# Six expert blocks with one shared down product of a weighted slot sum, and four head pieces moved from GpSimd to VectorE

## The chip, the cores and the metric

One core of one Trainium2 chip. The metric is the device time of one execution in microseconds (us), median of the runs given. In each core, TensorE (PE in the profile) does matrix products, VectorE (DVE) and ScalarE (ACT) elementwise work, GpSimd (POOL) slower elementwise work; each engine takes its instructions in the order in which they stand, and they wait for each other by semaphores. Products land in eight PSUM banks of 128 partitions x 512 float32.

## The reference, cut to what matters

A two-layer model on four sequences of 256 tokens by 256 features. Layer 0 has grouped attention (`attn_a`), an expert layer (`ffn`), an attention across the 16 heads of each token (`attn_b`), and the same expert layer again; layer 1 follows with a delta rule, two dense layers and an attention. The change touches the expert layer (called twice per sequence, so eight blocks) and the attention across heads.

```python
# expert layer, 8 experts, 2 of them chosen per token, F = 896, rank 32
rw, sel = top_k(softmax(x @ Wg.T), 2);  rw = rw / rw.sum()
base1 = x @ W1.T;  base3 = x @ W3.T
for k in range(2):
    mask = one_hot(sel[:, k], 8)
    x1 = base1 + lora1(mask);  x3 = base3 + lora3(mask)   # low-rank parts of the chosen expert
    x2 = silu(x1) * x3
    down  = x2 @ W2.T
    lora2 = (mask * (x2 @ A2.T)) @ B2                     # low-rank part of the down product
    out = out + (down + lora2) * rw[:, k]
# attn_b: for each token, softmax over its 16 heads
scores  = einsum('bshd,bstd->bsht', q, k) / sqrt(16)
attn    = einsum('bsht,bstd->bshd', softmax(scores), v)
```

## The kernel before, in words

The four sequences are named a, b, c, d (s = 0 to 3). Activations of a sequence are `X[s]` (2 tiles of 128 tokens x 256) and, transposed and normed, `XnT[s]`. The order of all work stands in one function, `program`: it calls `stage(name, k, s)` once for every step, and each engine runs through the same list and issues only its own part of a step (`table[name]`). So the order of an engine's queue is the order of this list.

**An expert block** (`experts(stage, k, s, beside)`) runs over seven tiles m of 128 of the 896 hidden features. `x_first` m is slot 0: eight products of 256 columns on TensorE, a Silu on ScalarE, a product on VectorE (`product`, result `x2T[s][:, 0, m]`). `x_second` m is slot 1, two steps of m later: four more products onto the same bank (the difference of the low-rank parts), then again Silu and product (`x2T[s][:, 1, m]`). The down products multiply each 128x128 block of `x2T` by 512 columns of `m_down`: 256 are W2, 256 are A2 of all experts. There are 2 slots x 2 token tiles x 7 tiles m = 28 of them. `down` on VectorE adds the W2 half, weighted by `rw`, to `X`, and masks the A2 half by `onehotw` into `am2` / `am2b`, which `lora_t` adds and `lora` multiplies by B2.

**Woven blocks.** In `middle` (once for a and b, once for c and d) two of the blocks run with the attention across heads of the other sequence beside them: block (0, b) with the heads of a, then block (1, a) with the heads of b; likewise (0, d) with c and (1, c) with d. I call the first kind W1 and the second W2; there are two of each. In them slot 0's down products are spread over the loop (`down_sum`), from m = 4 on. `token_heads(s)` says at which step of the block each part of the heads stands: 16 pieces (8 of scores, 8 of mixing, `head_scores` and `head_mix`), each made of a product of 128 x 1024 on GpSimd (`head_prod`) and a sum over 16 on VectorE. GpSimd may be four pieces ahead. The heads' result is transposed and projected on TensorE at the step "down10", behind the first of slot 1's two groups of down products (`head_out_t`, `head_out`).

**The other blocks**: (0, a) stands nearly alone; (0, c) has the first attention of d beside it; (1, b) and (1, d) have the start of the delta rule beside them.

PSUM banks are given out by `Ring`; `lanes` limits which banks a step may take. `claim` waits until the bank's former content is drained. TensorE's clock is granted by the chip; `warm` issues products without use where the engine would otherwise stand idle.

Of the kernel before, what the change touches and what calls it, by code (L numbers as in the profile page):

```python
# [8 lines left out]
ALU = mybir.AluOpType  # L9
# [3 lines left out]
P = 128  # L13
# [10 lines left out]
PIECES = 2 * NT * HP  # L24
NB = 4
# [73 lines left out]
def hybrid_kernel(nc, x_in, masks, packs, where, out):  # L99
    with ExitStack() as ctx:  # L100
# [206 lines left out]
        am_ready = each("am_ready")  # L307
        silu_ready = each("silu_ready")
# [102 lines left out]

        def lanes(name, k, s):
# [6 lines left out]
            if s % 2 == 0:  # L419
                return range(0, 3)  # L420
# [149 lines left out]
        def token_heads(s):  # L570
# [19 lines left out]
        def experts(stage, k, s, beside):  # L590
# [91 lines left out]
        def _(pe):  # L682
# [195 lines left out]

            def x_first(k, sm):
# [29 lines left out]
            def down(k, sia):  # L909
# [6 lines left out]
                for m in range(FT):  # L916
                    if i == 1 and a == 0:
                        wait_drained(pe, ("x", r, m))
                    last = mm(o[:, :], x2T[s][:, i, m, a * P:(a + 1) * P], wd[:, m, :], m == 0, m == FT - 1)
                last.then_inc(full[ring.bank(("down", r, i, a))], 1)  # L920

            def down_sum(k, sm):
# [4 lines left out]
                for a in range(NT):  # L927
                    o = claim(pe, ("down", r, 0, a)) if m == 0 else bank[ring.bank(("down", r, 0, a))]
                    last = mm(o[:, :], x2T[s][:, 0, m, a * P:(a + 1) * P], wd[:, m, :], m == 0, m == FT - 1)
# [296 lines left out]
            table = dict(head_prod=nothing, spread2=nothing, delta_sq=nothing, consts=nothing, top_exp=nothing, ffn_half=ffn_half, delta_expand=nothing, delta_diag=nothing, conv_tap=nothing, gates=nothing, down_sum=down_sum, angles=nothing, norm_x=nothing, norm_t=norm_t, latent=latent, kv=kv, kv_fold=kv_fold,  # L1226
# [19 lines left out]
        def _(act):  # L1246
# [70 lines left out]
            def silu(k, s, i, m):  # L1317
# [11 lines left out]
                act.activation(silu_x[s][:, n % SX, :], psum(key, T), ACT.Silu).then_inc(silu_ready[s], 1)  # L1329

# [163 lines left out]
            table = dict(head_prod=nothing, spread2=nothing, delta_sq=nothing, consts=nothing, top_exp=top_exp_, ffn_half=nothing, delta_expand=nothing, delta_diag=nothing, conv_tap=conv_tap, gates=nothing, down_sum=nothing, angles=angles, norm_x=nothing, norm_t=norm_t, latent=latent, kv=nothing, kv_fold=nothing,  # L1494
# [17 lines left out]
        def _(dve):  # L1512
# [177 lines left out]
            def gates(k, s):  # L1690
# [4 lines left out]
                link(dve.tensor_tensor(rw[s][:, 1, :], rw[s][:, 2, :], rw[s][:, 0, :], ALU.mult))  # L1695
                for a in range(NT):
# [3 lines left out]
                settle()  # L1700

# [32 lines left out]
            def down(k, sia):  # L1734
# [44 lines left out]
            def head_scores(_, sah):  # L1779
# [4 lines left out]
                dve.wait_ge(hprod_ready[s], nth(s, PIECES, p + 1))  # L1784
# [8 lines left out]
            def head_mix(_, sah):  # L1793
# [8 lines left out]
                dve.wait_ge(hprod_ready[s], nth(s, PIECES, p + 1))  # L1802
# [509 lines left out]
```

## Time and profile before

| | us |
|---|---|
| median of 3 runs (lowest, highest) | 1312.7 (1312.7, 1315.37) |
| the profiled execution | 1312.18 |
| its span in the trace | 1310.4 |
| TensorE busy | 1202.5 (92% of the span) |
| VectorE busy | 677.2 (52%) |
| ScalarE busy | 416.9 (32%) |
| GpSimd busy | 229.6 (18%) |

The page gives shares over the whole span; what a change in one stage is worth is read from the stage. The timeline gives every instruction with its start and duration, and in brackets how long its engine had been idle before it and what ended that. A float32 product of 256 or 512 columns shows as two instructions (two matmul records and two weight loads), so "x18" in a row of 128x512 products is nine of them; a transpose shows as one. Durations of single TensorE records overlap, so the price of a product is taken from a long row divided by its count.

### The profile page before, as it was taken

To read this page: it belongs to the slowest core of one execution; us is meant where nothing else is said; L and a number is where in the kernel's file an instruction comes from. 1 tells how busy PE (TensorE), PEld (TensorE's weight loads), DVE (VectorE), ACT (ScalarE), POOL (GpSimd) and SP (SyncE) were. 2 spreads that over 40 slices of the span, in tenths; PEclk is the share of its full clock that TensorE was granted. 3 is DMA by queue.
4 is the path that set the end of the run, shared out by engine and by line. 5 is a ranking of instruction groups with operands and counts; after the bars stand their busy time and mean duration, and the time that the engine had idled before them with its cause. 6 is when DMAs were issued, how large, how long until landed. Compare 5 with 4: busy or idle time off the path is not lost.

```text
span 1310.4 us, 17604 instructions
## 1 busy us (share of the span) xinstructions
PE 1202.5 (92%) x6865; PEld 916.2 (70%) x6865; DVE 677.2 (52%) x1661; ACT 416.9 (32%) x897; POOL 229.6 (18%) x133
## 2 busy tenths in 40 slices
PE   6889999999998989988787999999999989899888
PEld 5677675767866778667565776757678677786666
DVE  5753266664465456334634433666644655663351
ACT  3623021313222342433453431313133223424352
POOL 0000074560110210000000000836501102100000
PEclk9999999999999999989998999999999999998989
DMA  8200000000000000000000000000000000000000
GB/s 350 115 1 1 1 1 1 1 1 1 1 1 2 1 1 1 1 2 9 1 9 1 1 1 1 1 0 1 0 1 1 1 1 1 1 1 2 1 1 17
DMA packets 3570, 17.32 MB, mean 13 GB/s; under 512 B 288, under 2 KB 2464, under 8 KB 2976
## 3 DMA queue, kind: packets, MB, share of 16 engines
q1 hardware_dynamic: 2912, 14.12, 2.7%
q10 hardware_dynamic: 576, 2.08, 0.4%
q8 instruction: 55, 0.90, 0.3%
q14 instruction: 27, 0.22, 0.1%
HBM read 15.15 MB, written 1.05 MB: 12 GB/s over the span
## 4 chain that ended last, share of the span: by engine, by line
PE 70%; DVE 11%; issue 9%; ACT 6%; POOL 2%; DMA 0%; DVEq 0%; POOLq 0%; ACTq 0%
PE bank L684 66%; ACT scr L1278 3%; PE bank L701 2%; DVE XnT L1960 2%; DVE XnT L1962 1%; DVE scr L1552 1%; DVE stat L1544 1%; POOL rstd L2116 1%; DVE negmax L1634 1%; PE bank L802 1%; DVE X L1537 1%; PE bank L1089 1%; ACT scr L1256 1%; POOL fac L2116 1%; ACT XnT L1256 1%
## 5 line engine op out<-in xcount | busy, mean ns | idle before, releaser
L684 PE MATMUL bank<-pack,scr 128*128 128x512 f32 (+2 forms) x944 | 312.1, 483 | 8.5 <-ACT scr L1256 7.5
L684 PE MATMUL bank<-XnT,pack 128*128 128x256 f32 x1024 | 251.3, 385 | 11.9 <-ACT XnT L1256 7.1
L684 PEld LDWEIGHTS bank<-pack,scr 128*128 128x128 f32 x944 | 178.5, 193 | 114.9 <-issue 89.4
L684 PE MATMUL bank<-scr,pack 128*128 128x256 f32 x944 | 227.0, 380 | 1.3 <-DVE scr L1715 1.1
L684 PEld LDWEIGHTS bank<-XnT,pack 128*128 128x128 f32 x1024 | 191.7, 192 | 45.4 <-ACT XnT L1256 9.6
L684 PEld LDWEIGHTS bank<-scr,pack 128*128 128x128 f32 x944 | 178.1, 190 | 30.3 <-issue 4.4
L2138 POOL TENSOR_TENSOR scr<-scr 128x1024 f32<-128x1024 f32 x64 | 149.9, 2379 | 47.3 <-DVEq L1777 46.6
L2116 POOL TENSOR_TENSOR rstd<-veps,half 128x2 f32<-128x2 f32 x32 | 22.3, 698 | 750.2 <-DVE veps L1549 750.2
L1725 DVE TENSOR_TENSOR scr<-bank,scr 128x256 f32<-128x256 f32 x112 | 47.2, 423 | 149.5 <-ACT scr L1329 148.6
L1278 ACT ACTIVATE scr<-bank,negmax 128x256 f32<-128x256 f32 (+1 forms) x256 | 82.9, 445 | 92.5 <-DVE negmax L1634 92.5
L1329 ACT ACTIVATE scr<-bank 128x256 f32<-128x256 f32 x112 | 42.6, 384 | 210.5 <-PE bank L684 210.3
L1256 ACT ACTIVATE scr<-bank 128x512 f32<-128x512 f32 (+7 forms) x112 | 51.0, 474 | 176.8 <-PE bank L701 90.0
L684 PE MATMUL bank<-scr 32*128 32x128 f32 (+4 forms) x944 | 78.8, 322 | 1.3 <-ACT scr L1256 1.3
L684 PEld LDWEIGHTS bank<-scr 32*128 32x128 f32 (+2 forms) x944 | 65.7, 186 | 19.8 <-issue 9.0
L1632 DVE TENSOR_REDUCE negmax<-bank 128x2 f32<-128x512 f32 x64 | 43.8, 684 | 68.0 <-PE bank L684 68.0
L1256 ACT ACTIVATE mats<-bank 128x512 f32<-128x512 f32 (+1 forms) x80 | 42.6, 555 | 106.4 <-PE bank L1089 83.7
L1537 DVE TENSOR_TENSOR X<-bank,X 128x512 f32<-128x512 f32 x31 | 21.4, 691 | 94.2 <-PE bank L684 94.2
L802 PE MATMUL bank<-pack,scr 128*128 128x128 f32 x384 | 55.6, 295 | 8.2 <-ACT scr L1278 7.6
L701 PE MATMUL bank<-pack,scr 128*128 128x128 f32 x232 | 38.0, 292 | 24.5 <-DVE scr L1552 15.6
L684 PE MATMUL bank<-identb 128*128 128x512 bf16 x197 | 55.6, 383 | 5.0 <-DVE scr L1656 3.9
L802 PEld LDWEIGHTS bank<-pack,scr 128*128 128x128 f32 x384 | 46.5, 151 | 14.9 <-ACT scr L1278 11.6
L701 PEld LDWEIGHTS bank<-pack,scr 128*128 128x128 f32 x232 | 28.7, 149 | 39.9 <-issue 20.3
(178 smaller groups left out, 1384.9 us busy)
## 6 DMA issues: line engine op xcount, KB each, us to landing
pack<-pack_dram SPq DMA_DIRECT2D x1, 6152.0 KB, 17.5
pack<-pack_dram SPq DMA_DIRECT2D x1, 2180.0 KB, 29.6
pack<-pack_dram SPq DMA_DIRECT2D x1, 1595.0 KB, 23.5
X<-x SPq DMA_DIRECT2D x4, 256.0 KB, 16.9
pack<-pack_dram SPq DMA_DIRECT2D x1, 1024.0 KB, 20.3
pack<-pack_dram ACTq DMA_DIRECT2D x1, 975.5 KB, 6.3
pack<-pack_dram SPq DMA_DIRECT2D x1, 793.5 KB, 25.0
out_dram<-X SPq DMA_DIRECT2D x3, 256.0 KB, 2.1
```

Source lines behind the costliest of these rows:

```text
L684: return pe.matmul(o, l, r, start=start, stop=stop, skip_group_check=True)
L701: last = pe.transpose(o[:, t * T + a * P:t * T + a * P + P], src(t, a), ident)
L802: last = pe.transpose(o[:, (c - 4 * b) * P:(c - 4 * b + 1) * P], prob[s][:, u % PR, c * P:(c + 1) * P], ident)
L1256: act.activation(dst, src, func, **kw).then_inc(drain_of(key), 1)
L1278: ins = act.activation(prob[s][:, u % PR, j * HW + lo:j * HW + hi], psum(key, BANK)[:, lo:hi], ACT.Exp, bias=negmax[s][:, u % PR, tile, j: ...
L1329: act.activation(silu_x[s][:, n % SX, :], psum(key, T), ACT.Silu).then_inc(silu_ready[s], 1)
L1537: dve.tensor_tensor(xf, psum(key, n), xf, ALU.add).then_inc(drain_of(key), 1)
L1632: dve.tensor_reduce(negmax[s][:, u % PR, 1, 2 * h:2 * h + 2], o[:, :, P:HW], AX.X, ALU.max, negate=True).then_inc(max_ready[s], 1)
L1725: dve.tensor_tensor(x2T[s][:, i, m, :], psum(key, 2, T)[:, 1, :], silu_x[s][:, n % SX, :], ALU.mult)\
L1960: link(dve.tensor_tensor(t, rows16[:, 0:i + 1, :, i].rearrange("p j m -> p m j"), solved(s)[:, :, 0:i + 1], ALU.mult))
L2116: return pool.tensor_tensor(dst, src, half[:, 0:1].broadcast_to(shape) if len(shape) == 2 else half[:, 0:1].unsqueeze(1).broadcast_to(shap ...
L2138: pool.tensor_tensor(prod[s][:, hh], *pairs, ALU.mult).then_inc(hprod_ready[s], 1)
```

## The change

In six of the eight blocks (`joined`: all of k = 0, and (1, a) and (1, c)), the two slots share the W2 half of the down product. With rw0 and rw1 the weights and r = rw1 / rw0, the sum x2(0) + r x2(1) is formed in place of x2(1) and slot 1's down products take it; their result is weighted by rw0. Slot 0's 14 down products keep only the A2 half (256 columns instead of 512), and the mask of slot 0 becomes (onehot0 - onehot1) rw0, that of slot 1 onehot1 rw0, so that the A2 parts come out the same.

For this, `ratio_rows` copies r along 256 columns on VectorE at m = 0, TensorE turns it into rows with two products of 128 columns (`ratio`, behind `x_first` 1), ScalarE copies them to `ratio_t`, and GpSimd multiplies x2(1) by it and adds x2(0), two instructions of 128x256 for each m (`x_second` on GpSimd). The down products of slot 1 wait for `sum_ready`. VectorE no longer adds slot 0's part to `X` (two instructions fewer per block), and `gates` has one instruction more.

In the heads, the last four of the sixteen pieces (`AHEAD = 12`) get their product on VectorE right before its sum; GpSimd makes the first twelve. Two of the steps at which pieces stand are moved by one.

```diff
 PIECES = 2 * NT * HP
+AHEAD = PIECES - HP
...
+        def joined(k, s):
+            return k == 0 or s % 2 == 0
...
-                slots = ["f3", 3, "f4", 4, 4, "f5", 5, 5, "f6", 6, 6, "f7", 7, 7, 8, 8]
+                slots = ["f3", 3, "f4", 4, 4, "f5", 5, 5, "f6", 6, 6, "f7", 7, "f8", 8, 8]
...
-                slots = [1, "f2", 2, "f3", 3, 3, "f4", 4, "f5", 5, 5, "f6", 6, 6, "f7", 7]
+                slots = [1, "f2", 2, "f3", 3, 3, "f4", 4, "f5", 5, 5, "f6", 6, "f7", 7, "f8"]
...
-                if p + HP < len(pieces):
+                if p + HP < AHEAD:
                     beside[slot].append(("head_prod", 0, (s, p + HP)))
...
             for m in range(FT + 2):
+                if m == 0 and joined(k, s):
+                    stage("ratio_rows", k, s)
                 if m < FT and (m or (k == 0 and s % 2 == 0)):
                     stage("x_first", k, (s, m))
+                if m == 1 and joined(k, s):
+                    stage("ratio", k, s)
...
+            def ratio(k, s):
+                pe.wait_ge(ratio_ready[s], nth_sum(k, s, 1, 1))
+                o = claim(pe, ("ratio", (k, s)))
+                for a in range(NT):
+                    last = mm(o[:, a * P:(a + 1) * P], ratio_w[s][:, a, :], ident, True)
...
-                    last = mm(o[:, :], x2T[s][:, i, m, a * P:(a + 1) * P], wd[:, m, :], m == 0, m == FT - 1)
+                    if i == 1 and a == 0 and joined(k, s):
+                        pe.wait_ge(sum_ready[s], nth_sum(k, s, FT, m + 1))
+                    c0 = D if i == 0 and joined(k, s) else 0
+                    last = mm(o[:, c0:2 * D], x2T[s][:, i, m, a * P:(a + 1) * P], wd[:, m, c0:2 * D],
+                              m == 0, m == FT - 1)
...
+                if p < AHEAD:
+                    dve.wait_ge(hprod_ready[s], nth(s, AHEAD, p + 1))
+                else:
+                    wait_drained(dve, ("bv", s))
+                    link(dve.tensor_tensor(prod[s][:, hh], *pv_pairs(s, a, hh), ALU.mult))
                 dve.tensor_reduce(c[:, hh], prod[s][:, hh], AX.X, ALU.add).then_inc(hprod_read[s], 1)
...
+            def x_second(k, sm):
+                pool.wait_ge(x2_first[s], nth(s, 2 * FT, k * FT + m + 1))
+                wait_drained(pool, ("x", (k, s), m))
+                x2 = x2T[s][:, 1, m, :]
+                pool.tensor_tensor(x2, x2, ratio_t[s], ALU.mult).then_inc(scaled[s], 1)
+                pool.wait_ge(scaled[s], nth_sum(k, s, FT, m + 1))
+                pool.tensor_tensor(x2, x2, x2T[s][:, 0, m, :], ALU.add).then_inc(sum_ready[s], 1)
```

How the queues stand in the first W1 block. `scr0` holds the heads of a, `scr1` the block of b. GpSimd before has the sixteen head products in one run:

```order
L2116 TENSOR_TENSOR rstd<-veps,half 128x2 [waits var_ready0]
L2138 TENSOR_TENSOR scr<-scr 128x1024 [waits rot_ready0] x4
```

GpSimd with the change, from the block's first pair (L2191 multiplies by the ratio, L2193 adds slot 0; L2210 is a head product):

```order
L2191 TENSOR_TENSOR scr1<-scr1 128x256 [waits drained3,x2_first1,drained6]
L2193 TENSOR_TENSOR scr1<-scr1 128x256 [waits scaled1]
L2210 TENSOR_TENSOR scr0<-scr0 128x1024 [waits rot_ready0] x4
L2210 TENSOR_TENSOR scr0<-scr0 128x1024 [waits rot_ready0,hprod_read0]
L2191 TENSOR_TENSOR scr1<-scr1 128x256 [waits drained0,x2_first1]
L2193 TENSOR_TENSOR scr1<-scr1 128x256 [waits scaled1]
L2210 TENSOR_TENSOR scr0<-scr0 128x1024 [waits rot_ready0,hprod_read0] x2
L2191 TENSOR_TENSOR scr1<-scr1 128x256 [waits drained1,x2_first1]
L2193 TENSOR_TENSOR scr1<-scr1 128x256 [waits scaled1]
L2210 TENSOR_TENSOR scr0<-scr0 128x1024 [waits rot_ready0,hprod_read0]
```

What moved: the pairs of m = 1, 2 and 3 now stand between the head products, behind the fifth, seventh and tenth; two more products follow the pair of m = 3, then the pairs of m = 4, 5 and 6.

VectorE before, from the last piece but three of the heads of a (L1803 is the sum of a piece, L1725 the product x2 of the block of b, the last one being m = 6, slot 1):

```order
L1725 TENSOR_TENSOR scr1<-bank,scr1 128x256 [waits silu_ready1,dve_step]
L1799 TENSOR_REDUCE bsum0<-scr0 128x16 [waits b_exp0]
L1800 RECIPROCAL bmax0<-bsum0 128x16 [waits dve_step]
L1803 TENSOR_REDUCE scr0<-scr0 128x64 [waits hprod_ready0,dve_step]
L1803 TENSOR_REDUCE scr0<-scr0 128x64 [waits hprod_ready0]
L1725 TENSOR_TENSOR scr1<-bank,scr1 128x256 [waits silu_ready1]
L1803 TENSOR_REDUCE scr0<-scr0 128x64 [waits hprod_ready0] x2
L1807 TENSOR_TENSOR scr0<-scr0,bmax0 128x256 [waits hprod_read0]
```

and with the change (L1861 is the piece's product, L1862 its sum, L1779 the product x2):

```order
L1779 TENSOR_TENSOR scr1<-bank,scr1 128x256 [waits silu_ready1,dve_step]
L1854 TENSOR_REDUCE bsum0<-scr0 128x16 [waits b_exp0]
L1855 RECIPROCAL bmax0<-bsum0 128x16 [waits dve_step]
L1861 TENSOR_TENSOR scr0<-scr0 128x1024 [waits drained6,dve_step]
L1862 TENSOR_REDUCE scr0<-scr0 128x64 [waits dve_step]
L1861 TENSOR_TENSOR scr0<-scr0 128x1024 [waits drained6]
L1862 TENSOR_REDUCE scr0<-scr0 128x64 [waits dve_step]
L1779 TENSOR_TENSOR scr1<-bank,scr1 128x256 [waits silu_ready1]
L1861 TENSOR_TENSOR scr0<-scr0 128x1024 [waits drained6]
L1862 TENSOR_REDUCE scr0<-scr0 128x64 [waits dve_step]
```

What moved: the last product x2 stands behind two products and two sums of the heads, and two more of each follow it before L1866, the last scaling of the heads.

TensorE in the same block, from slot 0's last down products to the transposes of the heads' result, before:

```order
L684 MATMUL bank<-pack2,scr1 128x512 [waits x2_first1]
L684 MATMUL bank<-pack2,scr1 128x512
L684 MATMUL bank<-pack2,scr1 128x512 [waits drained2,drained1]
L684 MATMUL bank<-pack2,scr1 128x512 [waits drained3]
L684 MATMUL bank<-pack2,scr1 128x512 [waits drained0]
```

and with the change:

```order
L705 MATMUL bank<-pack2,scr1 128x256 [waits x2_first1]
L705 MATMUL bank<-pack2,scr1 128x256
L705 MATMUL bank<-pack2,scr1 128x512 [waits sum_ready1,drained3,drained2]
L705 MATMUL bank<-pack2,scr1 128x512 [waits sum_ready1,drained0]
L705 MATMUL bank<-pack2,scr1 128x512 [waits sum_ready1,drained1]
```

What moved: nothing in order; slot 0's down products have half the columns, and each of the first seven of slot 1 waits for GpSimd's sum. Behind them stand, as before, the transposes that wait for `bctx_ready`, the heads' result.

## Rows read from the trace of the kernel before

**Rows 1.** The page: shares of the chain that ended last, by engine.
```profile
PE 70%; DVE 11%; issue 9%; ACT 6%; POOL 2%; DMA 0%; DVEq 0%; POOLq 0%; ACTq 0%
```

**Rows 2.** Timeline of TensorE, blocks (0, a) and W1: start, duration, engine, operation [idle before].
```profile
123.93 24.20 PE L684 MATMUL bank<-pack,scr 128*128 128x512 f32 x56
...
159.09 1.03 PE L684 MATMUL bank<-XnT,pack 128*128 128x256 f32 x4
159.95 1.03 PE L684 MATMUL bank<-scr,pack 128*128 128x256 f32 x4
...
204.34 7.89 PE L684 MATMUL bank<-pack,scr 128*128 128x512 f32 x18
212.06 0.60 PE L701 MATMUL bank<-pack,scr 128*128 128x128 f32 x4
```

**Rows 3.** Window of W1's loop: length, busy PE, PEld, DVE, ACT, POOL, clock, DMA.
```profile
155.60:212.00 56.40, 56.40 (x215) 40.25 (x215) 37.60 (x61) 12.55 (x21) 38.16 (x17) 1.00 0.00 1
```

**Rows 4.** Timeline of GpSimd in the first W1 and W2.
```profile
172.05 37.51 POOL L2138 TENSOR_TENSOR scr<-scr 128x1024 f32<-128x1024 f32 x16 [13.41 <-DVEq L1777]
...
244.34 28.05 POOL L2138 TENSOR_TENSOR scr<-scr 128x1024 f32<-128x1024 f32 x12 [9.84 <-DVEq L1777]
```

**Rows 5.** Timeline of VectorE at the end of the heads of a (W1).
```profile
203.78 1.27 DVE L1807 TENSOR_TENSOR scr<-scr,bmax 128x256 f32<-128x256 f32 x1
...
206.15 2.35 DVE L1803 TENSOR_REDUCE scr<-scr 128x64 f32<-128x1024 f32 x2
208.41 0.41 DVE L1725 TENSOR_TENSOR scr<-bank,scr 128x256 f32<-128x256 f32 x1
208.74 2.33 DVE L1803 TENSOR_REDUCE scr<-scr 128x64 f32<-128x1024 f32 x2
211.11 0.42 DVE L1807 TENSOR_TENSOR scr<-scr,bmax 128x256 f32<-128x256 f32 x1
```

**Rows 6.** Groups by form: prices of operations near the new ones (count, busy, mean ns).
```profile
L684 PE MATMUL bank<-mats 128*128 128x128 f32 x288 | 34.5, 276 | 5.2 <-DVE mats L1984 5.2
...
L2157 POOL TENSOR_TENSOR mats<-pack,small 128x768 f32<-128x768 f32 x8 | 11.6, 1472 | 37.5 <-DVE small L1879 37.5
...
L1751 DVE TENSOR_TENSOR scr<-scr 128x512 f32<-128x512 f32 x8 | 5.5, 692 | 0.3
```

**Rows 7.** One line's instructions: duration ns min/median/max (VectorE, two GpSimd lines).
```profile
L1774 DVE TENSOR_TENSOR scr<-scr x8: 424/424/425, 168.5 to 896.7; 128x256 f32<-128x256 f32 x8
...
L2138 POOL TENSOR_TENSOR scr<-scr x64: 2324/2346/2550, 172.1 to 932.8; 128x1024 f32<-128x1024 f32 x64
...
L2176 POOL TENSOR_TENSOR scr<-scr,small x8: 830/830/832, 367.2 to 1120.0; 128x384 f32<-128x384 f32 x8
```

**Rows 8.** Timeline of VectorE where `ratio_rows` will follow: first in W1, then in (0, a).
```profile
158.68 0.86 DVE L1552 TENSOR_SCALAR scr<-X,mv,rstd 128x256 f32<-128x256 f32 x2 [0.81 <-POOL rstd L2116]
...
87.80 0.86 DVE L1552 TENSOR_SCALAR scr<-X,mv,rstd 128x256 f32<-128x256 f32 x2 [0.81 <-POOL rstd L2116]
```

**Rows 9.** Timelines at the heads' end in W2: VectorE's last scaling, TensorE's transposes.
```profile
286.00 0.42 DVE L1807 TENSOR_TENSOR scr<-scr,bmax 128x256 f32<-128x256 f32 x1
...
292.95 0.60 PE L701 MATMUL bank<-pack,scr 128*128 128x128 f32 x4
```

**Rows 10.** Timeline at the end of block (0, c): TensorE, then VectorE.
```profile
768.79 7.91 PE L684 MATMUL bank<-pack,scr 128*128 128x256 f32 x22
776.53 0.60 PE L701 MATMUL bank<-pack,scr 128*128 128x128 f32 x4
...
773.57 0.86 DVE L1552 TENSOR_SCALAR scr<-X,mv,rstd 128x256 f32<-128x256 f32 x2 [0.81 <-POOL rstd L2116]
```

**Rows 11.** TensorE's wait of 3.61 us, and windows behind it (clock third from last).
```profile
652.86 2.74 PE L802 MATMUL bank<-pack,scr 128*128 128x128 f32 x12 [3.61 <-ACT scr L1278]
...
653.00:654.00 1.00, 1.00 (x6) 0.81 (x5) 1.00 (x3) 1.00 (x5) 0.00 (x0) 0.50 0.07 16
...
656.00:657.00 1.00, 0.46 (x3) 0.06 (x1) 0.00 (x0) 1.00 (x5) 0.00 (x0) 0.82 0.00 0
```

More of the change, by code:

```diff
@@ L307, in hybrid_kernel @@
         am_ready = each("am_ready")
+        ratio_ready = each("ratio_ready")
+        scaled = each("scaled")
+        sum_ready = each("sum_ready")
         silu_ready = each("silu_ready")
@@ L410, in hybrid_kernel, with nth_sum @@
         halves, weave, summing, alone, scores_first = [False], [False], [False], [False], [False]
+        def joined(k, s):
+            return k == 0 or s % 2 == 0
+        JOINED = [[k for k in range(2) if joined(k, s)] for s in range(S)]
+        def nth_sum(k, s, per, n):
+            ks = JOINED[s % S]
+            return nth(s, per * len(ks), ks.index(k) * per + n)
         def lanes(name, k, s):
@@ L419, in lanes @@
             if s % 2 == 0:
-                return range(0, 3)
+                return range(3, 8) if name == "ratio" else range(0, 3)
             return dict(values=range(3, 4), scores=range(4, 8), weights=range(4, 8)).get(name, range(3, 8))
@@ L877, in spread @@
                     last.then_inc(full[ring.bank(("ex", r, i))], 1)
+            def ratio(k, s):
[3 more added lines that the diff above has]
+                    last = mm(o[:, a * P:(a + 1) * P], ratio_w[s][:, a, :], ident, True)
+                last.then_inc(full[ring.bank(("ratio", (k, s)))], 1)
             def x_first(k, sm):
@@ L928, in down_sum @@
                     o = claim(pe, ("down", r, 0, a)) if m == 0 else bank[ring.bank(("down", r, 0, a))]
-                    last = mm(o[:, :], x2T[s][:, 0, m, a * P:(a + 1) * P], wd[:, m, :], m == 0, m == FT - 1)
+                    c0 = D if joined(k, s) else 0
+                    last = mm(o[:, c0:2 * D], x2T[s][:, 0, m, a * P:(a + 1) * P], wd[:, m, c0:2 * D],
+                              m == 0, m == FT - 1)
                     if m == FT - 1:
@@ L1695, in gates @@
                 link(dve.tensor_tensor(rw[s][:, 1, :], rw[s][:, 2, :], rw[s][:, 0, :], ALU.mult))
+                if joined(k, s):
+                    link(dve.tensor_tensor(onehotw[s][:, :, 0, :], onehot[s][:, :, 0, :], onehot[s][:, :, 1, :],
+                                           ALU.subtract))
+                    for a in range(NT):
+                        step(dve.tensor_scalar(onehotw[s][:, a, 0, :], onehotw[s][:, a, 0, :], rw[s][:, 0, a:a + 1],
+                                               None, ALU.mult))
+                        step(dve.tensor_scalar(onehotw[s][:, a, 1, :], onehot[s][:, a, 1, :], rw[s][:, 0, a:a + 1],
+                                               None, ALU.mult))
+                    settle()
+                    return
                 for a in range(NT):
@@ L1739, in down @@
                 o = psum(key, 2, D)
-                link(dve.scalar_tensor_tensor(out=X[s][:, a, :], in0=o[:, 0, :],
-                                              scalar=rw[s][:, i, a:a + 1], in1=X[s][:, a, :],
-                                              op0=ALU.mult, op1=ALU.add))
+                if i or not joined(k, s):
+                    link(dve.scalar_tensor_tensor(out=X[s][:, a, :], in0=o[:, 0, :],
+                                                  scalar=rw[s][:, 0 if joined(k, s) else i, a:a + 1],
+                                                  in1=X[s][:, a, :], op0=ALU.mult, op1=ALU.add))
                 dst = am2 if i == 0 else am2b
```

28 lines of the change are left out of this document (21 added, 7 removed).

## The prediction

> **What bounds the kernel now.** I read the chain first: seven tenths of it are TensorE [rows 1], so work taken from TensorE counts, as long as TensorE is what its stage waits for. Then the windows of the stages that change. In the loop of a woven block TensorE is busy for all of its 56.4 us, but GpSimd is busy for 38.16 us and VectorE for 37.6 us of it [rows 3], and most of both lies late: GpSimd starts at 172.05, when the queries and keys are rotated, and makes sixteen products without a gap until 209.56 [rows 4]. VectorE sums the last piece and ends the heads at 211.53 [rows 5]. TensorE ends slot 1's first down products and turns to the heads' result at 212.06 [rows 2]. So three engines reach the end of a W1 block within half a microsecond of each other. TensorE alone sets the pace there only because the other two just keep up. In W2 VectorE is some 6.5 us ahead: the heads end at 286.42, and TensorE takes them up at 292.95 [rows 9].
>
> **What TensorE saves.** 56 records of 512 columns take 24.20 us, 0.864 for one product of two records; four records of 256 columns start 0.86 apart, 0.43 for one product [rows 2]. Each joined block narrows 14 products: 14 x 0.43 = 6.0 us, 36.2 us in six blocks. Added are two products of 128 columns, four records; 288 such records have 34.5 us [rows 6], so 0.12 x 4 = 0.5 us a block. How much of the net 33 us stays depends on what else is late at the end of each block.
>
> **What GpSimd gets.** Per joined block 14 instructions of 128x256 with two full inputs, no row shows this one. The nearest are 384 elements in 0.830 and 1024 in 2.346 us [rows 7] and 768 in 1.472 [rows 6]. The lowest price is by the element of the last, 1.92 ns x 256 = 0.49 us. Through 384 and 1024 (2.37 ns an element) lies 0.53; through 384 and 768 (1.67) lies 0.62; the 2.29 ns an element of the head product plus some start give 0.65. For the upper bound: GpSimd's small instruction on two elements, between the two steps of a norm, leaves VectorE idle for 0.81 us [rows 8], so a start of its own could cost some 0.4 us over the 0.59 of the elements, 0.97 in all. I take 0.65, and 0.04 for the second's wait: 1.34 us a pair, bounds 1.0 and 2.0.
>
> The Trainium skill (GPSIMD Engine Reference, section 3.1 "Elementwise — side-by-side cycle accounting") gives GpSimd about 2.6 cycles for an element of a two-input operation and says to leave elementwise work to VectorE; an estimate by it is 256 x 2.6 / 1.2 GHz = 0.55 us and a pair of 1.15. The trace's 2.346 us for 1024 lies near it (2.2 by the page). With that pair the sum below would be some 2.5 us lower; it speaks against the change no less.
>
> **What VectorE gets.** A head product of 128x1024 with both inputs in SBUF: 256 elements take 0.424 [rows 7] and 512 take 0.692 [rows 6], so 1024 take 0.692 + 2 x 0.268 = 1.23 us. It can't overlap its own sum, which waits for it (0.04). A sum costs 1.13 in a row: two lie between 206.15 and 208.41 [rows 5]. So each of the four last pieces is 2.4 us in place of 1.15, 5.0 us more a heads block. Taken away are two additions of 0.48 us behind the loop, which hid.
>
> **W1, step by step.** The copy of the ratio stands behind a norm on VectorE that ends at 159.54 [rows 8]; with 0.42 for the copy TensorE, ready at about 159.1 [rows 2], gets it at 160.0: a wait of 0.9, and 0.5 for the ratio products. All that follows in the loop starts 1.4 later, so GpSimd's first head product at 173.4. By the queue in the order rows, twelve products and three pairs stand up to the last product: 12 x 2.346 + 3 x 1.34 = 32.2, so 205.6. Then VectorE: sum of that piece 1.2 (206.8), scaling 0.4 and the product x2 of m = 5, 0.35 (207.6), the row sums 0.7 (208.3), two pieces 4.8 (213.1), the product x2 of m = 6, 0.4 (213.5), two pieces 4.8 (218.3), scaling 0.4: 218.7. TensorE starts the transposes at 218.8 and not at 212.06, **6.6 us later**, though it has 5.5 us less work. Its last down product before them waits for the pair of m = 6 (213.5 + 1.34, or 1.2 more if VectorE's product holds GpSimd up, as it is held up itself in the 1.27 us of a 0.42 us scaling [rows 5]); it ends by 217.1 and sets nothing. Behind the transposes all is as before. Bounds: 5.3 with pairs of 1.0, 9 with 2.0.
>
> **W2.** GpSimd starts at 244.34 [rows 4], 0.2 later for the copy. Its queue up to the twelfth product holds three pairs too: 244.5 + 32.2 = 276.7. VectorE: 277.9, scaling and x2 of m = 4 (278.6), row sums (279.4), two pieces (284.2), x2 (284.6), two pieces (289.4), scaling and x2 of m = 6: 290.1. The pair ends at 291.4, the last down product 0.86 later, and the transposes start at 292.3 and not 292.95: **0.7 earlier**, of 5.5. Bounds: 2.4 earlier and 2.2 later.
>
> **The clock.** In W1 TensorE idles some 8 us of the last 13 before the transposes, some 5 of it at a stretch; in W2 about 4. A wait of 3.61 us in the trace is followed by three microseconds at 0.50, 1.2 GHz, and back to 1.00 in the fourth [rows 11]: 3.5 us at half rate, which lose up to 1.75 us where TensorE has work. In W1 the idle goes on behind the first burst, so I take 2.5; in W2 the last down product, the transposes and the head projection run slow, 1.5. Bounds 0 and 3.5. The Trainium skill (TensorE: Matmul & The Clock Gate, "Why this matters for your kernels") warns of idle gaps between bursts of products, which set the clock back; the row agrees, and by the rule rival 2 below falls away.
>
> **(0, a)**: seven more narrow and seven narrow products stand between the loop and the first wait for a sum, 6.0 us, while the last pair takes 1.34: hidden. The ratio copy comes behind a norm that ends at 88.66 [rows 8] and costs 0.3 of wait: -6.0 + 0.5 + 0.3 = **-5.2**. **(0, c)**: TensorE's transposes for d's norm start at 776.53 and VectorE is ready at 774.43 [rows 10]; TensorE would be there at 773.5, so 0.9 of the first 3.0 is lost, the rest stands: -6.0 + 0.5 + 0.9 = **-4.6**.
>
> **Sum.** 2 x (6.6 + 2.5) + 2 x (-0.7 + 1.5) - 5.2 - 4.6 = 18.2 + 1.6 - 9.8 = +10.0. The profiled execution has 1312.18 (span 1310.4), 0.5 below the median; on the median of 1312.7 that gives 1322.7, **1322**.
>
> **Rivals.** (1) *The tails outlast TensorE, as summed*: 1322, from 1316 to 1328 as the clock and the pair vary. Chance 0.50. (2) *The clock stays up*: the single products between the waits keep it granted. The same sum without 8.0 is +2.0: 1315, within 0.2% of before. For it speaks that waits of 1 to 2 us elsewhere are passed at full clock; against it, [rows 11]. Chance 0.15. (3) *GpSimd's pair is cheap and the clock stays up*: 2 x 5.3 - 2 x 2.4 - 9.8 = -4.0: 1309, faster. It decides from pairs of some 1.1 us. Chance 0.14. (4) *Everything hides*: TensorE stays the bound and gains 36.2 - 3.0 - 0.9 = 32: 1280. It would need the heads to end 6 us before TensorE in W1; [rows 4, 5] show them ending level. Chance 0.06. (5) *GpSimd's small instructions cost 0.97 each*, W1 +9 + 3, W2 +2.2 + 2.5, 24.0 + 9.4 - 9.8 = +23.6: 1336. Chance 0.15, for lack of any row of that shape.
>
> **How the numbers follow.** The predicted time is that of the first, 1322. The range of 8 in 10 leaves out (4) and the far part of (5): 1307 to 1334. A measurement of this kernel tells 0.2% (2.6 us) from no change. Faster is (3), most of it, and (4): 0.20. Same is (2) and the rest of (3): 0.16. Slower is (1) and (5): 0.64.
>
> **What would show it.** Right: TensorE's new waits in W1 on GpSimd (L2193) and then on VectorE before the transposes, the transposes of W1 some 6 us and of W2 near 0 against before; GpSimd's 128x256 near 0.65; a granted clock of 0.5 behind these waits; a gain of about 5 us in (0, a). Wrong: TensorE still without a gap at the end of W1, or a 128x1024 product on VectorE far from 1.23 us.

## The result, and the profile with the change

The changed kernel has a median of 1332.33 us (1328.59 to 1333.02, 4 runs), the kernel before 1312.7 (1311.49 to 1315.37, 4 runs): a ratio of 1.0145, 95% interval 1.0125 to 1.0164. It is **slower by 19.6 us**. The prediction's direction and range held, its size did not: it had forecast a loss of 9.3 us (1322), about half of the measured one.

The page of the changed kernel, the shares of the chain that ended last, beside [rows 1] (TensorE 70%, VectorE 11%, GpSimd 2%):

```profile
PE 56%; DVE 18%; issue 10%; POOL 8%; ACT 6%; DMA 0%; DVEq 0%; POOLq 0%; ACTq 0%
```

TensorE's waits by line that ended them (us in total, times, longest). The first row has no counterpart in the kernel before; the second, on the norms, had 15.6 us in the kernel before.

```profile
PE bank L705 <- POOL scr L2193: 25.9, 10, 4.8
PE bank L722 <- DVE scr L1591: 16.0, 10, 7.1
```

TensorE's timeline with the change at the end of the first W1, which answers to the last two rows of [rows 2]:

```profile
199.34 4.46 PE L705 MATMUL bank<-pack,scr 128*128 128x256 f32 x12
204.77 1.10 PE L705 MATMUL bank<-pack,scr 128*128 128x512 f32 x2 [0.98 <-POOL scr L2193]
208.04 2.05 PE L705 MATMUL bank<-pack,scr 128*128 128x512 f32 x2 [2.18 <-POOL scr L2193]
213.95 2.05 PE L705 MATMUL bank<-pack,scr 128*128 128x512 f32 x2 [3.85 <-POOL scr L2193]
216.65 1.11 PE L722 MATMUL bank<-pack,scr 128*128 128x128 f32 x4 [0.66 <-DVE scr L1866]
218.45 10.63 PE L705 MATMUL bank<-pack,scr 128*128 128x256 f32 x22 [0.69 <-ACT scr L1290]
```

Where TensorE had one run of products there are now single ones between waits for GpSimd's sums. One product of two records takes 1.10 us in the first such row and 2.05 in the next two. The granted clock says why; windows of the same stretch (length; busy time of PE, PEld, DVE, ACT, POOL; clock; DMA):

```profile
204.00:208.00 4.00, 1.10 (x2) 0.30 (x2) 3.83 (x7) 0.00 (x0) 2.94 (x3) 0.84 0.00 0
208.00:214.00 6.00, 2.10 (x3) 0.59 (x3) 5.93 (x7) 0.00 (x0) 2.29 (x2) 0.50 0.00 0
214.00:222.00 8.00, 6.66 (x14) 3.99 (x15) 4.20 (x7) 0.60 (x1) 0.00 (x0) 0.50 0.00 0
222.00:224.00 2.00, 2.00 (x4) 0.91 (x3) 1.56 (x5) 0.00 (x0) 0.00 (x0) 0.55 0.00 0
224.00:226.00 2.00, 2.00 (x6) 0.84 (x5) 1.11 (x5) 0.00 (x0) 0.71 (x1) 1.00 0.00 0
```

From 208 to some 223 us the clock is at 0.50, 1.2 GHz. TensorE is busy for 2.10 of the first six of these microseconds; from 216.65 on it has work again and does it at half speed.

**A ledger by stretches.** Fifty of TensorE's transposes of four records can be found in every trace, in the same order. The distance between two of them, less the distance in the kernel before, tells what a stretch gained or lost (times of the kernel before in brackets). Each ledger here is that of one profiled execution:

| stretch | change, us | forecast |
|---|---|---|
| (0, a) (76.75 to 149.96) | -4.65 | -5.2 |
| W1 up to the heads' transposes (149.96 to 212.06), both | +7.28, +7.34 | +6.6 each |
| W1 behind them (212.06 to 221.19), both | +3.14, +2.92 | +2.5 each |
| W2 up to the transposes (235.54 to 292.95), both | +1.24, +1.39 | -0.7 each |
| W2 behind them (292.95 to 302.08), both | +3.14, +2.97 | +1.5 each |
| (0, c) (701.89 to 803.18) | -4.44 | -4.6 |
| all the rest | +0.34 | 0 |
| sum | +20.7 | +10.0 |

The +0.34 of the rest is what is left of larger parts, in stretches that the change doesn't touch: +2.97 (69.60 to 76.75), +3.21 (1074.18 to 1122.89), -2.64 (508.37 to 571.27) and smaller ones. The granted clock differs there: 0.64 in the changed kernel from 72 to 79 us, and 0.69 in the kernel before from 560 to 571, with 1.00 at the same work in the other trace. That they nearly cancel is chance.

### The profile page after: what moved, and what is told of

It reads as the page before. It is cut to its first block, busy times and chain, and to the rows that moved or that the text cites. A ratio compares the mean times of both kernels' runs of the same rounds, so it can differ in the third digit from the quotient of the medians.

```text
span 1331.1 us, 17824 instructions
## 1 busy us (share of the span) xinstructions
PE 1189.5 (89%) x6889; PEld 925.4 (70%) x6889; DVE 691.4 (52%) x1677; ACT 418.3 (31%) x903; POOL 258.8 (19%) x201
## 4 chain that ended last, share of the span: by engine, by line
PE 56%; DVE 18%; issue 10%; POOL 8%; ACT 6%; DMA 0%; DVEq 0%; POOLq 0%; ACTq 0%
PE bank L705 52%; POOL scr L2210 5%; ACT scr L1312 3%; DVE scr L1862 2%; PE bank L722 2%; DVE XnT L2019 2%; DVE scr L1861 1%; DVE XnT L2021 1%; DVE scr L1591 1%; DVE stat L1583 1%; POOL rstd L2175 1%; DVE X L1576 1%; DVE negmax L1673 1%; DVE scr L1822 1%; PE bank L823 1%
## 5 line engine op out<-in xcount | busy, mean ns | idle before, releaser
L705 PE MATMUL bank<-pack,scr 128*128 128x256 f32 (+3 forms) x968 | 293.8, 455 | 36.3 <-POOL scr L2193 25.9
L705 PEld LDWEIGHTS bank<-pack,scr 128*128 128x128 f32 x968 | 185.6, 198 | 123.6 <-issue 89.6
L705 PE MATMUL bank<-XnT,pack 128*128 128x256 f32 x1024 | 258.2, 393 | 12.3 <-ACT XnT L1290 7.1
L705 PEld LDWEIGHTS bank<-XnT,pack 128*128 128x128 f32 x1024 | 195.7, 196 | 44.2 <-ACT XnT L1290 9.5
L1779 DVE TENSOR_TENSOR scr<-bank,scr 128x256 f32<-128x256 f32 x112 | 47.1, 423 | 142.6 <-ACT scr L1363 141.6
L2210 POOL TENSOR_TENSOR scr<-scr 128x1024 f32<-128x1024 f32 x48 | 112.0, 2362 | 29.0 <-DVEq L1832 29.0
L2191 POOL TENSOR_TENSOR scr<-scr 128x256 f32<-128x256 f32 x42 | 34.5, 821 | 131.7 <-DVE scr L1779 131.7
L722 PEld LDWEIGHTS bank<-pack,scr 128*128 128x128 f32 x232 | 29.2, 152 | 43.5 <-issue 20.6
```

The source lines that it names most:

```text
L705: return pe.matmul(o, l, r, start=start, stop=stop, skip_group_check=True)
L722: last = pe.transpose(o[:, t * T + a * P:t * T + a * P + P], src(t, a), ident)
L1779: dve.tensor_tensor(x2T[s][:, i, m, :], psum(key, 2, T)[:, 1, :], silu_x[s][:, n % SX, :], ALU.mult)\
L2191: pool.tensor_tensor(x2, x2, ratio_t[s], ALU.mult).then_inc(scaled[s], 1)
L2210: pool.tensor_tensor(prod[s][:, hh], *pairs, ALU.mult).then_inc(hprod_ready[s], 1)
```

## Experiments

The first theory was the prediction's, with the sizes of this ledger: TensorE's saving is real, but VectorE with its four longer pieces and GpSimd with its pairs end after it in the woven blocks, and the clock falls in the waits that this makes. The rivals were that one of the two parts is the cause alone, or the clock alone. "The table" in the expectations is a list of the woven block's instructions by engine, with durations and waits from the traces, worked through.

**Each part by itself.** e1 joins only the two blocks beside which no heads stand:

```diff
-            return k == 0 or s % 2 == 0
+            return k == 0 and s % 2 == 0
-AHEAD = PIECES - HP
+AHEAD = PIECES          # and the slots of before
```

> Only the blocks (0,a) and (0,c) are joined; the heads keep their sixteen GpSimd products and their slots of before, and W1 and W2 are as before. The ledger of the two profiles gives (0,a) -4.65 us and (0,c) -4.9 us. My theory (each block's change stands on its own, since TensorE meets a wait on the others between any two of them): 1312.7 - 9.5 = 1303.2, range 1301 to 1306. Rival: the gain of (0,a) and (0,c) is partly taken back by what follows (W1 starts earlier against the same VectorE and GpSimd work, or a fall of the clock as in (1,a) at 70 us): 1306 to 1312.

Measured: 1300.54 us, ratio 0.9919 (0.9892 to 0.9945). In its ledger (0, a) has -4.67 and (0, c) -4.46, the woven blocks 0.01 or less. The time is just under my range. So the change has a good part, worth 9.1 us, and nothing takes it back; the rest of what e1 gains lies in stretches that it doesn't touch (more on those below).

e2 has only the heads' part, e3 only the pairs:

```diff
-            return k == 0 or s % 2 == 0
+            return False            # e2; AHEAD and slots as in the change
-AHEAD = PIECES - HP
+AHEAD = PIECES                      # e3; slots of before, six blocks joined as in the change
```

> No block is joined; the last four products of the heads are VectorE's, whole, in the change's slots. My theory: the two parts of the change each make VectorE and GpSimd late at the same place and don't add up. A hand-made table of the woven block, with the traces' durations, gives W1 +3.4 us each, all of it a longer wait in front of the heads' transposes (3.4 us), and W2 0; if the clock falls to 1.2 GHz behind that wait, +3 us more in each W1: 1319.5 to 1326. Rival A (the moved products are the whole loss of the woven blocks, some 29 us): over 1335. Rival B (GpSimd's pairs are the whole loss): 1313.

> Six blocks joined as in the change, but all sixteen products of the heads stay on GpSimd in the slots of before. My theory: the table gives W1 +7.6, W2 0 up to the transposes, the clock's fall 3 us in each of the four woven blocks and 0.4 for the ratio copy's wait in W1, less 9.5 in (0,a) and (0,c): +18 to +20, so 1331 to 1333, no better than the change. Rival A (VectorE's moved products are the cause): W1 and W2 keep the saving of 6.0 us that TensorE has, 1280 to 1300. Rival B (the pairs are the cause, and the move of the four products made it better): over 1338.

Measured: e2 1321.03, ratio 1.0053 (1.0031 to 1.0076); e3 1328.34, ratio 1.0123 (1.0099 to 1.0146). Their ledgers, with the change's beside them, first and second block of each kind:

| us | e2, heads | e3, pairs | both (the change) |
|---|---|---|---|
| W1 up to the transposes | 3.79, 3.84 | 9.78, 9.80 | 7.28, 7.34 |
| W1 behind them | 2.57, 2.41 | 2.27, 0.39 | 3.14, 2.92 |
| W2 up to the transposes | 0.00, 0.81 | 1.18, 1.53 | 1.24, 1.39 |
| W2 behind them | 0, 0 | 0, 0 | 3.14, 2.97 |

Either part makes the woven blocks slower by itself: 13.4 us with the heads' part, 25.0 with the pairs, 29.4 with both. So they don't add, and the pairs alone make most of the loss: the interval of e3's ratio overlaps the change's. e3 came out below my 1331 to 1333, because the clock cost it 2.7 us behind the transposes where I had 12. In W1 the pairs alone are the worst, since GpSimd then has sixteen head products and all pairs, one behind the other. Its timeline in e3:

```profile
204.95 6.91 POOL L2210 TENSOR_TENSOR scr<-scr 128x1024 f32<-128x1024 f32 x3
211.80 0.74 POOL L2191 TENSOR_TENSOR scr<-scr 128x256 f32<-128x256 f32 x1
212.62 0.72 POOL L2193 TENSOR_TENSOR scr<-scr 128x256 f32<-128x256 f32 x1
213.30 0.91 POOL L2191 TENSOR_TENSOR scr<-scr 128x256 f32<-128x256 f32 x1
214.29 0.72 POOL L2193 TENSOR_TENSOR scr<-scr 128x256 f32<-128x256 f32 x1
```

Moving four products to VectorE takes 2.5 us of that back (9.8 to 7.3) and costs more elsewhere: in W2, where VectorE had 6.5 us of slack [rows 9], it brings nothing up to the transposes, and the work behind them now runs at half clock. (e3 has its fall in the first W2 ahead of them: four records of 128x512 take 3.36 us there, from 298.18 on, at a clock of 0.50; the transposes behind them take 0.60.) e3's table value of +7.6 in W1 (8.0 with the ratio copy) was 1.8 too low.

**How much is GpSimd's width.** e4 keeps every instruction and wait of the change and cuts GpSimd's to two columns:

```diff
-                pool.tensor_tensor(x2, x2, ratio_t[s], ALU.mult)
+                pool.tensor_tensor(x2[:, 0:2], x2[:, 0:2], ratio_t[s][:, 0:2], ALU.mult)
-                pool.tensor_tensor(x2, x2, x2T[s][:, 0, m, :], ALU.add)
+                pool.tensor_tensor(x2[:, 0:2], x2[:, 0:2], x2T[s][:, 0, m, 0:2], ALU.add)
```

> As the change, but GpSimd scales and adds only 2 of the 256 columns of each of the seven sums of a block, so 254 columns of each sum are left out; all instructions and waits stay. My theory: the table with 0.1 us in place of 0.725 us gives W1 +2.2 and W2 -2.8 up to the transposes, less 9.5 in (0,a) and (0,c): 1301.5 with the clock kept, up to 1308 if it still falls behind the longer waits in front of the transposes. Rival A (VectorE is the cause, not GpSimd's time): within 4 us of the change, 1328 to 1333. Rival C (the fixed cost of GpSimd's start and its waits is the cause, not the width): 1315 to 1325.

Measured: 1323.89, ratio 1.0076 (1.0054 to 1.0099), well above my 1301 to 1308. By the total rival C would have it, and the ledger shows that it is not so simple: W1 up to the transposes is +3.88 and +3.97, W2 -0.70 and -1.30; 2.37, 2.96, 0.45 and 2.62 lie behind them; and (0, c) has +4.27 in place of -4.44, 8.7 us more. So the width is worth 3.4 us in each W1 and 1.9 and 2.7 in W2, some 11 us in all. Of the 12.2 us behind the transposes 8.4 stayed, and (0, c) took 8.7 back. That one is the clock, in a stretch that e4 leaves as it is in the change. Two windows of e4 from the start of that stretch:

```profile
700.00:711.00 11.00, 10.75 (x36) 9.18 (x37) 5.39 (x21) 1.20 (x2) 0.00 (x0) 0.54 0.00 0
...
722.00:733.00 11.00, 11.00 (x54) 8.71 (x53) 6.75 (x20) 4.26 (x10) 0.00 (x0) 0.71 0.00 1
```

What stays in W1 up to the transposes is near e2's 3.8. TensorE and then VectorE in e4's W1:

```profile
207.00 2.05 PE L705 MATMUL bank<-pack,scr 128*128 128x512 f32 x2 [5.59 <-POOL scr L2193]
210.68 1.12 PE L722 MATMUL bank<-pack,scr 128*128 128x128 f32 x4 [1.63 <-DVE scr L1866]
...
200.19 1.23 DVE L1861 TENSOR_TENSOR scr<-scr 128x1024 f32<-128x1024 f32 x1
201.46 1.22 DVE L1862 TENSOR_REDUCE scr<-scr 128x64 f32<-128x1024 f32 x1
202.59 1.22 DVE L1861 TENSOR_TENSOR scr<-scr 128x1024 f32<-128x1024 f32 x1
203.84 1.22 DVE L1862 TENSOR_REDUCE scr<-scr 128x64 f32<-128x1024 f32 x1
204.98 0.41 DVE L1779 TENSOR_TENSOR scr<-bank,scr 128x256 f32<-128x256 f32 x1
```

The wait of 5.59 us is put down to GpSimd's L2193, but GpSimd needs only 1.32 us from the start of its pair to the end of it: it stood idle for 5.37 us until the product x2 of m = 6 at 204.98, and that stood behind two whole pieces of the heads in VectorE's queue. The releaser of a wait is not its cause; here the cause is two steps back, in another engine's order. My table was too low by 1.3 us in W1 and by 1.5 to 2.1 in W2; in W2 the last product in front of the transposes at half rate, 1.84 us for 0.86, is 1.0 of that.

**VectorE's order.** e6 tests that directly, with the full width:

```diff
-   "f6", 6, 6, "f7", 7, "f8", 8, 8]        # heads of a, c
+   "f6", 6, 6, 7, 7, 8, 8, 8]
-   "f6", 6, "f7", 7, "f8"]                 # heads of b, d
+   "f6", 6, 7, 8, 8]
```

> The change, but in VectorE's order the x2 products of m = 5 and m = 6 stand ahead of the last pieces of the heads that the change has ahead of them (the slots f7 and f8 become 7 and 8); same work, same waits. My theory: GpSimd's last pair starts earlier, and the heads' end stays where VectorE's total puts it. The hand-made table gives W1 0 (the wait moves from the sum to the transposes, 4.4 us there), W2 -2.5 us each; the clock's fall in W2 (3.1 us each) goes too, that in W1 stays: 1332.3 - 5 - 6.2 = 1321, range 1318 to 1326. Rival A (GpSimd's own backlog sets the sums, not the place of VectorE's product): 1330 to 1333, no change. Rival B (the clock falls in W2 all the same): 1327.

Measured: 1320.32, ratio 1.0062 (1.0040 to 1.0084), 12 us better than the change (11 by the ratios). W1 up to the transposes stays at +7.35 and +7.41: the sum comes earlier, but the heads' end is what counts, and the wait moves there. W2 goes from +1.24 and +1.39 to **-2.28 and -2.22**. TensorE in the first W1, then the first W2:

```profile
209.25 2.05 PE L705 MATMUL bank<-pack,scr 128*128 128x512 f32 x2 [4.08 <-POOL scr L2193]
214.34 1.12 PE L722 MATMUL bank<-pack,scr 128*128 128x128 f32 x4 [3.04 <-DVE scr L1866]
...
293.68 1.10 PE L705 MATMUL bank<-pack,scr 128*128 128x512 f32 x2 [1.23 <-POOL scr L2193]
296.39 0.66 PE L722 MATMUL bank<-pack,scr 128*128 128x128 f32 x4 [1.61 <-DVE scr L1866]
297.73 8.00 PE L705 MATMUL bank<-pack,scr 128*128 128x256 f32 x22 [0.69 <-ACT scr L1290]
```

and W2 with the change:

```profile
295.29 1.10 PE L705 MATMUL bank<-pack,scr 128*128 128x512 f32 x2 [1.68 <-POOL scr L2193]
300.08 2.05 PE L705 MATMUL bank<-pack,scr 128*128 128x512 f32 x2 [3.70 <-POOL scr L2193]
301.92 1.06 PE L722 MATMUL bank<-pack,scr 128*128 128x128 f32 x4
303.67 10.69 PE L705 MATMUL bank<-pack,scr 128*128 128x256 f32 x22 [0.69 <-ACT scr L1290]
```

So VectorE's order was worth 3.5 and 3.6 us in the two W2, and where the waits shrank the clock stayed up in the first W2 (8.00 us for the 22 records). In the second it fell all the same (3.01 us behind the transposes), so rival B was right for one of the two.

**The clock by itself.** e5 is the change with products without use in TensorE's waits; VectorE and GpSimd have the same work in the same order.

```diff
+                    if m in hot:                      # W1 {4: 3, 5: 8, 6: 18, 7: 5}, W2 {5: 6, 6: 15, 7: 3}
+                        if m == min(hot):
+                            wait_drained(pe, ("x", r, 4))
+                            spare = claim(pe, ("down", r, 1, 1))
+                        warm(spare, hot[m])
                     if i == 1 and a == 0:
                         wait_drained(pe, ("x", r, m))
...
+                if FT in hot:                         # in front of the heads' transposes
+                    warm(spare, hot[FT])
```

> The change as it is, with TensorE kept busy by products of zeros-and-ones in an unused bank where it waits in W1 and W2: 3, 8, 18 and 5 products of 128x512 bf16 in front of the sums 4, 5, 6 and the heads' transposes of W1, 6, 15 and 3 in front of sums 5, 6 and the transposes of W2. Nothing of VectorE's and GpSimd's work is changed. My theory: the clock's fall is the one part of the loss that isn't VectorE's or GpSimd's time: the stretches behind the transposes go back to 9.1 us (3.1 less in each of four), those in front of them keep +7.3 and +1.2: 1332.3 - 12.5 = 1320, range 1317 to 1323. Rival A (the stretches behind the transposes are longer for another reason, TensorE's own queue or VectorE's backlog): 1330 to 1335. Rival B (the added products delay the sums by what they take beyond the waits): over 1335.

Measured: 1317.99, ratio 1.0050 (1.0032 to 1.0068), 14 us under the change's median; 12.5 by the ratios. The four stretches behind the transposes are at +0.05, +0.06, 0.00 and 0.00 against before (with the change +3.14, +2.92, +3.14 and +2.97), the ones in front of them are where they were (+7.28, +7.38, +1.09, +1.19). TensorE in W1, and then its windows:

```profile
206.23 4.05 PE L706 MATMUL bank<-identb 128*128 128x512 bf16 x18
211.21 1.10 PE L706 MATMUL bank<-pack,scr 128*128 128x512 f32 x2 [0.93 <-POOL scr L2207]
212.14 1.24 PE L706 MATMUL bank<-identb 128*128 128x512 bf16 x5
213.91 0.66 PE L723 MATMUL bank<-pack,scr 128*128 128x128 f32 x4 [0.53 <-DVE scr L1880]
215.25 8.00 PE L706 MATMUL bank<-pack,scr 128*128 128x256 f32 x22 [0.69 <-ACT scr L1304]
```

```profile
206.00:212.00 6.00, 5.07 (x21) 2.06 (x20) 5.93 (x6) 0.00 (x0) 2.30 (x2) 1.00 0.00 0
212.00:218.00 6.00, 4.78 (x21) 2.87 (x20) 4.07 (x8) 0.60 (x1) 0.00 (x0) 1.00 0.01 3
```

VectorE and GpSimd are as late as before, only the clock is different, and behind the transposes it is worth 12 us of the 20. In W2 the three products in front of the transposes took 0.64 us with nothing to wait for, and so took back most of the 0.9 us that the last product at full rate had brought.

The Trainium skill (TensorE: Matmul & The Clock Gate, "Why this matters for your kernels") warns of such idle gaps between bursts; e5's rows agree, at 3 us for each of the four places. It doesn't settle which gaps do it: e6's two W2 have nearly the same gaps, and the clock fell behind one of the two (last section).

**A better version.** The runs say what to keep: (0, a) and (0, c), W2 with the right order, W1 not at all. e7 does that, e8 moves two products where e7 moves four, e9 is e7 with 4 and 5 products without use in W2's two waits.

```diff
-            return k == 0 or s % 2 == 0
+            return s % 2 == 0
-AHEAD = PIECES - HP
+AHEAD = (PIECES, PIECES - 4)    # heads of a, c; of b, d. e8: PIECES - 2
                                 # slots: a, c as before; b, d as in e6
+HOT = ({}, {6: 4, 7: 5})        # e9 alone, used as in e5
```

> Joined are (0,a), (0,c) and W2, not W1. The heads of a and c keep sixteen GpSimd products and the slots of before; those of b and d (beside W2) have twelve, and their last three pieces stand behind VectorE's x2 products of m = 5 and 6. My theory: e1's 1300.5, less 2.8 us in each W2 (table): 1295, range 1292 to 1298, if the clock stays up behind a wait of 2 us in front of the transposes. Rival (the clock falls behind it, 3 us each): 1298 to 1302, no gain on e1. Rival B (each place where GpSimd comes between VectorE and TensorE costs more than the table has, as e4's W1 did, +1.7): 1298 to 1300.

> As e7, but only the last two products of the heads of b and d are VectorE's. My theory: the table gives -2.9 us in each W2 with shorter waits (0.7, 1.6 and 0.3 us in place of 0.8 and 2.0), so that the clock is the likelier to stay up: 1295, range 1292 to 1297. Rival (GpSimd's two further products of 2.35 us stand ahead of its last pairs and make them later than the table has): 1299 to 1304.

> e7 (joined are (0,a), (0,c) and W2; the last pieces of the heads of b and d behind the x2 products) with products in an unused bank in W2's waits: 4 in front of sum 6, 5 in front of the heads' transposes. In e7 the stretches behind W2's transposes were 1.6 and 3.0 us longer than in the kernel before. My theory: the clock accounts for both; 1294.8 - 4.6 = 1290, range 1288 to 1293. Rival (no more than a chance difference in the clock of that one profiled run, which the median doesn't have): 1293 to 1296.

Measured: e7 1294.78, ratio 0.9888 (0.9855 to 0.9921); e8 1296.91, ratio 0.9888 (0.9865 to 0.9911); e9 1297.15, ratio 0.9893 (0.9855 to 0.9930). W2 up to the transposes is -2.27 and -2.18 in e7, -1.70 and -2.36 in e8, -2.26 and -2.20 in e9. Behind them e7 loses 1.63 and 3.02, e8 0.45 and 0.07, e9 0.05 and 0.06. So W2 brought 2.2 us where my table had 2.8, and in e7 the clock fell behind both: its theory held in the total alone, with luck in untouched stretches. e9's products do at their place what was expected (4.5 us less than e7), yet its total missed my 1288 to 1293 and is no better than e7's. The difference lies in stretches where both kernels have the same instructions: e9 is 8 us longer there, 3.1 of them between 1058.29 and 1110.14 in its trace. A window of e7 and one of e9, at nearly the same work there:

```profile
1075.00:1091.00 16.00, 15.43 (x97) 11.71 (x96) 7.29 (x18) 5.74 (x17) 3.86 (x3) 1.00 0.00 0
```

```profile
1074.00:1090.00 16.00, 15.43 (x88) 11.56 (x87) 7.29 (x18) 5.55 (x17) 4.24 (x3) 0.89 0.00 0
```

TensorE is busy for 15.43 us of 16 in both, and gets 97 records done at a clock of 1.00 and 88 at 0.89. The three versions can't be told apart from each other, nor surely from e1 (0.9919, 0.9892 to 0.9945); all are faster than both kernels, against the one before in the same runs by 11 to 15 us by the ratios (12 to 19 by the medians).

## Why the prediction came out low

**What bounds the kernel, TensorE's saving.** Right: three engines end W1 level, and the new waits stand where they were forecast. In (0, a) the 56 down records take 18.22 us where [rows 2] has 24.20: 6.0 us, as forecast, and (0, a) and (0, c) came out at -4.65 and -4.44 for -5.2 and -4.6. In (0, a) the ratio copy's wait and its two products cost 0.63 together, forecast 0.8, and a later wait on VectorE's product (0.44 us, at 107.15) was not in the sum; with what surrounds it that is 0.7.

**GpSimd's pair.** Taken as 0.65 an instruction, measured 0.725, with 0.80 from the first's start to the second's:

```profile
L2193 POOL TENSOR_TENSOR scr<-scr x42: 721/725/1590, 99.0 to 961.8; 128x256 f32<-128x256 f32 x42
```

A pair is 1.52 us for 1.34, inside the bounds. The estimate of 0.55 us by the Trainium skill's page (GPSIMD Engine Reference, section 3.1) is a quarter below the row. By the page the sum would have been still lower. The bounds for dearer and cheaper pairs were not worked out cleanly: W1 waits for three pairs and W2 for four, so pairs of 1.0 us give 5.6 later and 2.1 earlier, not 5.3 and 2.4, and rival 3 comes to -2.8 us in place of -4.0; it did not come true either way.

**VectorE's product**: 1.22 us for 1.23 [rows 6, 7].

**W1**: +7.3 for +6.6. The chain is there as written: VectorE waits 1.08 us for GpSimd's last head product (L2210), and then has no gap until the last scaling. From that product's end (203.14) to the scaling's (216.59) are 13.45 us, forecast 13.1.

```profile
203.17 1.22 DVE L1862 TENSOR_REDUCE scr<-scr 128x64 f32<-128x1024 f32 x1 [1.08 <-POOL scr L2210]
...
210.87 0.41 DVE L1779 TENSOR_TENSOR scr<-bank,scr 128x256 f32<-128x256 f32 x1
...
216.17 0.42 DVE L1866 TENSOR_TENSOR scr<-scr,bmax 128x256 f32<-128x256 f32 x1
```

**W2: a mis-sized term**, -0.7 forecast, +1.24 and +1.39 measured. VectorE's last x2 came where it should: 7.73 us taken off, by which the block starts later, it ends at 290.54, forecast 290.1. What failed stands behind it. GpSimd in W2:

```profile
298.41 0.72 POOL L2191 TENSOR_TENSOR scr<-scr 128x256 f32<-128x256 f32 x1 [3.27 <-DVE scr L1779]
299.21 0.72 POOL L2193 TENSOR_TENSOR scr<-scr 128x256 f32<-128x256 f32 x1
```

From VectorE's end at 298.27 to TensorE's product at 300.08 are 1.81 us, forecast 1.34 for the bare pair; and from that product to the transposes 1.84 us, forecast 0.86. So 0.4 are VectorE's, 0.5 the pair's with its hand-overs, and 1.0 the clock's, of 1.9. The forecast had named the last down product as slow, but its 1.5 us for the clock was too small to hold both this and what lies behind.

**The clock: the term that was mis-sized most.** Forecast 2.5 in W1 and 1.5 in W2 (8.0 in all), measured 3.14, 2.92, 3.14, 2.97 behind the transposes (12.2), and 1.0 more inside each W2. I had read from [rows 11] that a wait of 3.61 us is followed by 3.5 us at half rate, and sized the loss behind these waits from that length. That step failed: in W1 single products between waits don't bring the clock back, and it stays at 0.50 for 15 us; in the first W2 it is at 0.50 from 299 to 309 us, nine of them behind a last wait of 3.70 us that was hardly longer than the one in [rows 11]. The bound of 3.5 us held in W1; in W2, where the term was to hold the last down product too, it measured 4.1 and 3.9 and lay outside. e5 shows the part behind the transposes. Why the clock came back so much later here than in [rows 11] no run shows.

**The parts together.** W2 is short by 2.0 us up to the transposes and by 1.6 behind them, W1 by 0.7 and 0.5, in two blocks each: 9.6 of the 10.3 by which these stretches were short, and (0, a) has 0.6. Of these the clock is 6.1 (14.1 for 8.0). Rival 2 (the clock stays up, 1315) is what e5 makes by force, at 1318. Rival 5 (a GpSimd instruction of 0.97, 1336) has the nearest total and the wrong mechanism: the row has 0.725.

## What to carry to other kernels

Where three engines end a stage within half a microsecond of each other, work taken from one of them brings nothing while the others get more, and each engine that now stands between two others costs hand-overs; where one engine was alone at the end, as in (0, a) and (0, c), the same edit gave nearly all it promised. So apply such an edit stage by stage, and leave it out where the other engines end level. Before a queue gets longer pieces, look for the short result that another engine waits for and put it ahead of them: in W2 that alone turned +1.3 us into -2.2. A wait of some microseconds on TensorE, also one that is broken up by single products, can cost twice: once for itself and once for the work behind it, at half the clock (12 us here, in four places). The waits alone didn't tell where it would.

## What the runs showed of the hardware that I had not expected

**Whether the clock falls is not set by the waits alone.** In e6 the first and second W2 have nearly the same waits (1.23 and 1.61 us, 1.29 and 1.61). The second, beside the first shown above:

```profile
949.65 1.10 PE L705 MATMUL bank<-pack,scr 128*128 128x512 f32 x2 [1.29 <-POOL scr L2193]
952.36 0.98 PE L722 MATMUL bank<-pack,scr 128*128 128x128 f32 x4 [1.61 <-DVE scr L1866]
```

The four transposes take 0.98 us here and 0.66 there, and the stretch behind them 3.01 us more. What decides it I can't say. The same happens in stretches that no kernel here changes: between the marks at 1074.18 and 1122.89 (times of the kernel before) the change, e4, e8 and e9 are 3.1 to 3.2 us longer than the kernel before, and e1, e2, e3, e5, e6 and e7 are equal to it within 0.01 us. e4's fall in (0, c) is another. e3's two W1 are 9.8 us late alike, and the stretches behind their transposes are 2.3 and 0.4 us longer. So a total of this kernel carries several microseconds of chance that depend on no edit (the six times of e7 alone lie between 1293.45 and 1307.47), and the ledger by stretches told the theories apart where the totals of e4 and e9 would have misled.

**GpSimd and VectorE hold each other up.** GpSimd's addition at 206.31 in W1 takes 1.59 us in place of 0.72 beside VectorE's product of 128x1024 at 206.01; its multiplication at 211.43 takes 1.57 beside the product at 211.21. They end 0.59 and 0.57 us after VectorE's product. The other way round it is little: VectorE's product at 206.01, which starts during a GpSimd instruction, takes 1.30 us for 1.22.

```profile
206.01 1.30 DVE L1861 TENSOR_TENSOR scr<-scr 128x1024 f32<-128x1024 f32 x1
...
206.31 1.59 POOL L2193 TENSOR_TENSOR scr<-scr 128x256 f32<-128x256 f32 x1
...
211.43 1.57 POOL L2191 TENSOR_TENSOR scr<-scr 128x256 f32<-128x256 f32 x1 [3.53 <-DVE scr L1779]
```

Even an instruction of two columns took 1.04 us at that place in e4, and 0.20 elsewhere. So the products moved to VectorE cost GpSimd 0.85 us at each of these places, the second one straight ahead of the sum for which TensorE waits. The prediction had allowed for this there (1.2 us), and rightly let it set nothing in W1: the heads' end comes 0.66 us after that product.
